# A wait of its own for each of 64 scatters, and eleven of sixteen output tiles summed by TensorE

## The reference

```python
x = x + _layernorm(_L0_attn_ref(_layernorm(x), Wq, Wk, Wv, Wo))
x = x + _layernorm(_L0_ffn_ref(_layernorm(x), gate_w, gate_up, down, shared_gate_up, ...))
# _L0_ffn_ref(x):
routing_probs = jax.nn.softmax(x @ gate_w.T)
topk_w, topk_idx = jax.lax.top_k(routing_probs, K)            # K = 4 of E = 16
shared = _silu_mul(x @ shared_gate_up.T, SI) @ shared_down.T  # SI = 704
shared = shared * jax.nn.sigmoid(x @ shared_gate_vec.T)
# over the 16 experts: acc + (silu_mul(x @ w_gu.T, 176) @ w_d.T) * combine[:, e]
return shared + sparse
```

## Time and profile before

| | us |
|---|---|
| median of 3 runs | 626.38 (625.57 to 630.11) |
| the profiled execution | 625.45, of which 623.7 is the span from first to last instruction |
| PE busy | 502.3 of 623.7 |
| DVE, ACT, POOL busy | 414.5, 342.6, 325.2 |
| mean granted TensorE clock | 0.926 |

### The profile page before, as it was taken

One profiled execution on the slowest core, in us unless ns is written; L12 is line 12 of the kernel. 1 busy time (PEld: TensorE's weight loads), 2 busy tenths in 40 slices (PEclk: granted clock), 3 DMA queues, 4 the chain that ended last, 5 costly groups with the idle time before them and its releaser, 6 DMA issues.

```text
span 623.7 us, 11475 instructions
## 1 busy us (share of the span) xinstructions
PE 502.3 (81%) x3484; PEld 386.3 (62%) x3484; DVE 414.5 (66%) x1011; ACT 342.6 (55%) x701; POOL 325.2 (52%) x357
## 2 busy tenths in 40 slices
PE   2738899899999998878887783898999999999300
PEld 1614455656565453367667663787999999999300
DVE  6529878888788857259646732566997666665287
ACT  2141576696577557754442311656886666666223
POOL 5431543481464215326266575605668887777544
PEclk9859899999999999989898996898999999999755
DMA  7241651534063440340036232639998888887593
GB/s 270 66 136 51 193 185 53 166 130 152 24 212 108 128 135 2 100 141 1 18 125 227 107 108 90 204 89 267 253 250 139 147 146 148 141 129 101 79 374 143
DMA packets 71033, 86.33 MB, mean 138 GB/s; under 512 B 6272, under 2 KB 64192, under 8 KB 70976
## 3 DMA queue, kind: packets, MB, share of 16 engines
q1 hardware_dynamic: 53264, 63.15, 32.7%
q0 software_dynamic: 14448, 19.31, 17.4%
q10 hardware_dynamic: 3264, 3.15, 1.4%
HBM read 33.68 MB, written 39.12 MB: 117 GB/s over the span
## 4 chain that ended last, share of the span: by engine, by line
PE 30%; DVE 10%; issue 5%; DMA 4%; ACT 3%; another core or an unknown queue 3%; POOL 1%; ACTq 0%; POOLq 0%; SPq 0%; DVEq 0%
PE gate_ps L1938 11%; PE y_ps L1961 7%; PE y_ps L1914 3%; PE m_ps L1856 2%; PE gate_ps L938 2%; DMA acc_dram<-yout,xin 2%; DVE total L1769 2%; PE up_ps L938 1%; PE up_ps L1949 1%; PE up_ps L1950 1%; DVE hid L1665 1%; DVE ystats L1771 1%; DMA added<-acc_dram 1%; DVE hid_lo L1695 1%
## 5 line engine op out<-in xcount | busy, mean ns | idle before, releaser
L1276 POOL DMA_INDIRECT acc_dram<-yout,xin x79 | 124.5, 1576 | 59.9 <-ACT yout L1409 28.4
L702 DVE TENSOR_REDUCE nmax<-a_ps 128x2 f32<-128x768 f32 (+3 forms) x88 | 96.0, 1121 | 13.7 <-PE a_ps L837 13.2
L587 ACT ACTIVATE probs<-a_ps 128x1024 f32<-128x1024 f32 (+1 forms) x96 | 81.3, 883 | 28.4 <-PE a_ps L859 24.4
L488 POOL TENSOR_SCALAR_AFFINE_SELECT probs<-probs 128x256 f32<-128x256 f32 (+1 forms) x96 | 47.0, 500 | 91.4 <-ACT probs L587 91.3
L1264 POOL DMA_INDIRECT xs_dram<-xrow,idx x64 | 63.8, 997 | 42.1 <-issue 18.9
L1938 PE MATMUL gate_ps<-w_all,rxT_hi 128*128 x316 | 78.0, 329 | 1.3 <-issue 1.3
L1743 DVE TENSOR_TENSOR h<-rsilu,gate_ps 128x176 f32<-128x176 f32 x79 | 26.6, 337 | 50.6 <-ACT rsilu L1394 41.4
L1961 PE MATMUL y_ps<-w_all,hT_hi 128*128 x237 | 57.6, 311 | 0.7 <-DVE hT_lo L1750 0.7
L1938 PEld LDWEIGHTS gate_ps<-w_all,rxT_hi 128*128 128x128 f32 x316 | 52.5, 190 | 3.1 <-issue 2.5
L832 PE MATMUL a_ps<-KTt,QT 96*128 96x128 bf16 (+3 forms) x256 | 49.9, 305 | 4.4 <-DVE nmax L702 2.2
L1938 PE MATMUL gate_ps<-w_all,rxT_lo 128*128 x158 | 51.3, 325 | 0.0
(11 more groups left out here) (291 smaller groups left out, 1334.0 us busy)
## 6 DMA issues: line engine op xcount, KB each, us to landing
xin<-xs_dram SPq DMA_DIRECT2D x79, 136.5 KB
xs_dram<-zeros SPq DMA_DIRECT2D x7, 1365.0 KB, 6.9
w_all<-in_wex_dram SPq DMA_DIRECT2D x16, 480.0 KB
QT<-parts SPq DMA_DIRECT2D x48, 128.0 KB
KTt<-parts SPq DMA_DIRECT2D x48, 128.0 KB
acc_dram<-zeros SPq DMA_DIRECT2D x6, 640.0 KB, 8.2
added<-acc_dram ACTq DMA_DIRECT2D x12, 256.0 KB, 9.1
x_all<-in_x_dram SPq DMA_DIRECT2D x4, 512.0 KB, 8.0
```

Of the source, the lines that this page charges most:

```text
L488: pool.affine_select(out=pr, in_=pr, pattern=[[0, nh], [1, P]], compare_op=ALU.is_ge, fill=0.0, base=0, channel_multiplier=-1).then_inc(ma ...
L587: nc.scalar.activation(dst, src, ACT.Exp, scale=float(DH) ** -0.5).then_inc(a_act, 1)
L702: nc.vector.tensor_reduce(nmax[:, i, h:h + nh].rearrange("p (b h) -> p b h", h=hb), src, AX.X, ALU.max, negate=True).then_inc(a_dve, 1)
L1276: pool.indirect_dma_start(out=acc[a][:, :], out_offset=bass.IndirectOffsetOnAxis(ap=xin[:, p % XIN, XROW - 1:XROW].bitcast(mybir.dt.uint32 ...
```

## The change

Two parts. In the dense stage each scatter n now has its own wait: an event number 7 + n * 15 // 16 is split into a step s and one of three events, 0: gate_ready, 1: hid_done, 2: down_done, each >= s + 1. In the last stage TensorE adds the three parts of eleven tiles in PSUM, by three products with the identity, into places that earlier stages no longer use; these are the odd tiles and 2, 6 and 10. VectorE keeps the additions of tiles 0, 4, 8, 12 and 14.

```diff
+PACE_FROM = 7
+        half_summed = sem("half_summed")
+        sum_places = [ps[:, j, k * D:(k + 1) * D] for ps in (gate_ps, up_ps, m_ps) for j in range(2)
+                      for k in range(2)] + [y_ps[:, j, :] for j in range(TB)]
+        def by_pe(i):
+            return i % 2 == 1 or i // 2 in (1, 3, 5)
+        def summed(i):
+            return sum_places[i] if by_pe(i) else total[:, i, :]
                     for k in range(K):
                         n = i * K + k
-                        if k == 0:
-                            pool.wait_ge(down_done, 4 + i)
+                        step, event = divmod(PACE_FROM + n * 15 // 16, 3)
+                        pool.wait_ge((gate_ready, hid_done, down_done)[event], step + 1)
                         pool.indirect_dma_start(
...
-                    ins = nc.scalar.activation(total[:, i, :], total[:, i, :], ACT.Identity,
+                    ins = nc.scalar.activation(total[:, i, :], summed(i), ACT.Identity,
...
-                dve.wait_ge(total_in[h], 16 * ACCS)
-                for a in range(ACCS - 1):
-                    link(nc.vector.tensor_tensor(total[:, tiles, :], total[:, tiles, :], added[:, a, tiles, :], ALU.add))
+                if not by_pe(tiles.start):
+                    dve.wait_ge(total_in[h], 16 * ACCS)
+                    for a in range(ACCS - 1):
+                        to = total[:, tiles.start, :]
+                        link(nc.vector.tensor_tensor(to, to, added[:, a, tiles.start, :], ALU.add))
+                dve.wait_ge(half_summed, h + 1)
                 for i in range(tiles.start, tiles.stop):
-                    ins = nc.vector.bn_stats(stats[:, i, :], total[:, i, :])
+                    ins = nc.vector.bn_stats(stats[:, i, :], summed(i))
...
+            for n in range(2 * B):
+                pe.wait_ge(total_in[n], 16 * ACCS)
+                for i in range(n * TB // 2, (n + 1) * TB // 2):
+                    if by_pe(i):
+                        for a in range(ACCS):
+                            part = added[:, a - 1, i, :] if a else total[:, i, :]
+                            ins = nc.tensor.matmul(sum_places[i], ident[:], part, start=a == 0, stop=a == ACCS - 1,
+                                                   skip_group_check=True)
+                ins.then_inc(half_summed, 1)
```

## The result

The changed kernel takes 621.98 us in the median of 14 runs (618.19 to 625.86) where the kernel before takes 626.47 (14 runs): ratio 0.9912, 95% interval 0.9887 to 0.9938. That is a gain of 0.9% by the ratio; the forecast was 617, a gain of 1.5%. The profiled execution took 622.44, against 625.45 before: 3.01 less.

What follows compares the result with a forecast made beforehand. Dense stage taken as held by TensorE events arriving late during unbroken scatters, last stage as bound by VectorE. Dense stage -6.5 and last stage -2.7 sum to -9.2: 625.45 to 616.3, plus 0.9 for the median, 617; range 612 to 622.

Steps and rivals of the forecast that it cites:

- Late events: Dense stage: TensorE's semaphore events arrive late from about the seventh unbroken scatter on; the backlog passes when GpSimd pauses.
- on time: Rival, dense stage: no late event outlasts the pipeline's slack, GpSimd is the bound; -16.6 with the last stage, 610; chance 0.2.
- First run, +2.2: Dense stage, first run of scatters: 14 scatters instead of 12, so ScalarE goes on 2.2 us later.
- Second run, -3.1: Dense stage, second run: stops at scatter 24 after ten scatters, late events pass at 342.5; gives back 3.1 us.
- Third and fourth, -9.1: Dense stage: fourth run stops at scatter 43 after 11 scatters, not 16; gate_up(18) starts near 375, not 383.79; -9.1 us together.
- The end, 3.6 lost: Dense stage's end: the late last scatters delay the pages, so the transposes before down(23) wait, costing 3.6 us.
- a bound of 1.9: Dense stage: scatters beside VectorE's weight splits may run longer; charged nothing, upper bound 5 x 0.37 = 1.9 us.
- the last scatter is late: Rival, dense stage: late events stay and the last scatter is late; 627 to 631, say 629; chance 0.28.
- The last stage, -2.7: Last stage: TensorE's sums spare VectorE additions, h = 1 starts 1.8 later; the last operation starts 2.7 us earlier, at 617.9.
- The low-clock rival: Rival, last stage: TensorE stays at the low clock, +6.5 instead of -2.7, 626 us; chance 0.1.
- the signs named ahead: Profile signs: runs of 14, 10, 11; last scatter within 2.5 of down(21); transposes waiting 3 to 4; full clock from 599.

Runs made afterwards that it cites:

- e9: Changed kernel with scatters waiting for nothing of the dense stage, on a chip with late events: 660.43 us against 628.48 for the kernel before, ratio 1.0524.
- e5: Changed kernel with scatters spread evenly (event 13 + 3n/4), on a chip with late events: 622.4 us against 629.94 for the kernel before, ratio 0.9849.
- e3: Changed kernel without the scatters' waits on the dense stage, on a chip without late events: 608.4 us, ratio 0.9957 to the kernel before.
- e7: Changed kernel with scatters waiting for nothing of the dense stage, again on a chip without late events: 607.79 us, ratio 0.9957 to the kernel before.
- e11: Changed kernel, dense-stage waits replaced by a wait for the previous scatter's landing before every eighth, chip with late events: 624.85 us, ratio 0.9936 to the kernel before.
- e10: Kernel before with the new scatter waits alone, on a chip with late events: 624.55 us against 630.31 for the kernel before, ratio 0.992.

## Why the prediction was right, and where not

The gain has the sign forecast. Its size is about half: the sum was -9.2, where the medians give -4.5 and the profiled executions -3.0, a third. That 621.98 lies inside the range of 612 to 622, by 0.02 us, is luck; the profiled execution, 622.44, lies outside.

*Late events.* The mechanism holds, as e9 shows, with a condition that one trace couldn't show: it belongs to some chips. The rival "on time", 610 with GpSimd as the bound, describes the other kind (607.8 to 609.0 with the sums, in the kernels without waits for landings), but there the kernel before takes 611 too.

*First run, +2.2:* 14 scatters as forecast, silu(8) 3.0 late instead of 2.2.

*Second run, -3.1:* it stopped after ten, as forecast. ScalarE's output of batch 1 then came at 349.76, 1.0 later than before (348.72), so 2.0 of the 3.0 came back, not 3.1.

*Third and fourth, -9.1:* here the forecast had left out a customer of late events. The second table (`idx_ready` 2) came at 359.31, 1.9 later than before, where I let the run start 0.9 earlier, at 356.5. silu(16) was then 5.7 late. The stop at scatter 43 came after eleven scatters, and the copy for batch 3 started 3.6 after its transposes' end (371.76), 9.6 less than before; I had 7 to 9. But those transposes themselves came 3.5 later than before, so the copy started at 375.34, where I had 371.9 to 374.3, and gate_up(18) at 377.94, not near 375. At down(21) all this leaves 6.7 of the 10.0 forecast: 403.49 against 410.19.

*The end, 3.6 lost:* the largest single miss. It lost 5.4, in two parts. The wait for the pages was 4.24 instead of 3.6. And the sum had nothing for the clock behind that wait: transposes and down(23) took 3.1 at a granted clock of 0.50, where I had 2.0.

The wait is longer because of the last scatter. I let it follow down(21) by 2.1 and so start at 402.3. With down(21) at 403.49 that would be 405.6; it started at 406.35, and no event held it: the last eleven scatters run from 391.17 with no gap of over 0.31. GpSimd's row was late by itself. I had followed scatter 43's stop and the last two scatters, not the pause of 2.29 ahead of scatter 53, nor the length of the row behind it. Four of its scatters took 1.80, 1.33, 1.84 and 1.32 instead of 0.97, 2.4 together, charged at nothing in the sum with a bound of 1.9. Without them, by the same 2.1 behind down(21), the event would still have held the last scatter until about 405.6; so by this estimate only 0.8 of the 2.4 reached the end. The rival "the last scatter is late" had this half right. All four begin within a split on VectorE (timeline of the changed kernel):

```profile
390.97 1.15 DVE L1658 TENSOR_TENSOR w_all<-w_all 128x960 fp32r<-128x960 f32 x1
...
393.89 1.15 DVE L1658 TENSOR_TENSOR w_all<-w_all 128x960 fp32r<-128x960 f32 x1
...
398.59 1.15 DVE L1658 TENSOR_TENSOR w_all<-w_all 128x960 fp32r<-128x960 f32 x1
...
402.76 1.15 DVE L1658 TENSOR_TENSOR w_all<-w_all 128x960 fp32r<-128x960 f32 x1
```

The Trainium skill, GPSIMD Engine Reference, "Key points", names such instructions of VectorE, with two inputs in SBUF, as contending with GpSimd. This trace agrees, with exceptions. Of the 14 scatters that begin within a subtraction of two tiles in SBUF (L1658, L1707) eight take over 1.05, among them all five that begin within a split of the weights; of the other 50 only the first does. Before, the split at 401.11 left the scatter at 401.14 at 0.97, so the rule names where a scatter can be long, not that it will be.

*The last stage, -2.7:* 2.1 measured, 23.36 against 25.49. VectorE's timeline of the changed kernel (compare):

```profile
594.22 0.88 DVE L1783 TENSOR_TENSOR total<-total,added 128x256 f32<-128x256 f32 x2 [12.50 <-DMA added<-acc_dram]
...
600.60 0.76 DVE L1786 BATCH_NORM_STATS2 ystats<-gate_ps 128x6 f32<-128x256 f32 x2 [2.29 <-PE gate_ps L1985]
...
617.58 0.69 DVE L1803 TENSOR_TENSOR total<-total,x_all 128x512 f32<-128x512 f32 x1 [0.52 <-ACT total L1436]
```

TensorE's:

```profile
594.24 1.22 PE L1985 MATMUL gate_ps<-total,ident 128*128 128x256 f32 x2 [11.51 <-DMA added<-acc_dram]
...
596.96 1.06 PE L1985 MATMUL gate_ps<-total,ident 128*128 128x256 f32 x2
...
599.11 0.59 PE L1985 MATMUL gate_ps<-total,ident 128*128 128x256 f32 x2
...
600.40 0.59 PE L1985 MATMUL up_ps<-total,ident 128*128 128x256 f32 x2
```

At the full clock a tile of three products, each in two records, takes 1.29 (599.11 to 600.40), 0.43 each: as forecast. The first tile, at the low clock, takes 2.72 (594.24 to 596.96), 0.91 each instead of 0.85, and the statistics of h = 1 start 6.4 after the first load instead of 5.7. That is the 0.6 that was missing; from there the steps are as forecast (16.98 to the last operation, where I had 17.1). The profiles with the sums have 22.8 to 24.5 for the last stage, those without 25.5 to 25.9, on chips of both kinds. The low-clock rival is refuted by the page's 0.8 in the last slices and by these records.

Of the signs named ahead, the runs of scatters, the clock, TensorE's records and VectorE's half batches were as expected; the last scatter was 2.9 behind down(21), not within 2.5, the transposes waited 4.2, not 3 to 4, and the copy for batch 3 gained 9.6, not 7 to 9.

What stays open: why both parts together gave 0.9912 in the result when the waits alone gave 0.992 on another chip with late events; the product of the two parts, 0.992 x 0.996 = 0.988, lies just below the interval. The two parts never ran together beside one part alone on a chip with late events. The single runs of the changed kernel spread over 7.7 us and those of the kernel before over 7.9, so one profile of each says little about where the waits fall in the others. The evenly spread kernel (e5, 0.9849) is the best found, by a profile that doesn't show why; it never ran beside the changed kernel.

## What to carry to other kernels

Where one engine's row of small DMAs has to be through before a later stage can load, add up that row itself, with its pauses and its long members, and set it against the dense work beside it: each pause that helps the others moves the last one back. When a wait is moved to let others go ahead, follow every consumer of the late events, tables and splits too, to the last instruction of the waiting queue. And a change tuned on one chip's stalls can be worth nothing on another: measure the kernel before on the same chip each time.

## What the runs showed of the hardware

Chips differ by 2.5 to 3% for the same program of one core, and here the profiles show one mechanism in the difference. On two chips 64 indirect DMAs back to back disturb nothing (e3, e7, both with spans of about 606). On the others they slow TensorE's own issue to one product in 2.09 us and hold its events back by up to 17.8 us (e9), and a pause of GpSimd of 2.3 to 4.0 clears most of this whatever it waits for (e11; events up to 3.9 late are left). The same program costs 52.6 more there (e9 and e7).

The traces differ in one more thing. Each scatter adds 16 to one of two semaphores, so 512 to each in all. The traces from the chips without late events hold 510 to 513 increments of each; those of the chips with late events hold 137 and 175 (before), 144 and 178 (after), 131 and 177 (e5), 96 and 97 (e9), 150 and 191 (e10), 204 and 247 (e11). So on these chips increments are lost from the record. The loss isn't of the scatters alone, and it doesn't go with stalls everywhere. Counted over all semaphores, up to 300 us the traces of both kinds hold the same (2729 before and in e7), and so again in the last stage (794 and 795). Between the dense stage's end and the last stage, where GpSimd scatters the experts' results, they hold 2614 before and 3826 in e7; yet that stretch takes 179.5 and 180.1 us. Records are thus missing in both stretches with indirect DMAs, but time is lost only in the dense stage. The runs listed come with a span and a granted clock each, so all of them were recorded; whether a run that isn't recorded has the stalls, and so whether they are the chip's or the recorder's, no run here shows. The Trainium skill, NOTIFIC — the notification-queue block, "7.1 Overflow: three behaviours, one of which stalls the engine", says that the block's internal pipeline holds its producers back rather than lose a record inside the block, which would be such a way from records to stalled engines; no run here tests it.
